# One block for attention and the gated stage, down products of six tiles chunk by chunk, and three x products placed right after the scan

## The chip, the core and the metric

The kernel runs on one core of a Trainium2 chip, in one launch. The metric is device time in microseconds. TensorE (PE, with its weight loads as PEld), VectorE (DVE), ScalarE (ACT), GpSimd (POOL) and SyncE (SP, which issues the transfers) run side by side and meet only at semaphores. The order of each engine's instructions is the order in which the Python code issues them.

## What is computed

1024 tokens (two sequences of 512) with 512 channels go through four stages. After each one its input is added and the sum is layer-normalised.

```
x = layernorm(x + mamba2(x))        # projections z, x, B, C; conv of 4 taps + silu; selective scan in 128-token
                                    # chunks, 8 groups; gating with silu(z); group norm; output projection
x = layernorm(x + x @ dequant(W))   # one 512x512 linear layer
x = layernorm(x + attention(x))     # 32 heads, 8 key/value heads, rotary, causal
g = silu(x @ gate.T * gs);  u = x @ up.T * us          # 1376 inner channels
x = layernorm(x + ((g * u) @ down.T) * ds)             # the gated stage
```

Operands that need more than 16 bits of mantissa are split in a leading and a remaining 16-bit half; a product of two such operands is three matmuls (lines 59, 60, 61), one with an exact operand two.

## The kernel before

**The mixer** (the first stage) works in *slots*. A tile is 128 of a group's 1024 channels for one sequence; there are 8 groups, 2 sequences, 8 tiles each, so 128 tiles, and a *unit* is the 8 tiles of one group and sequence. `slots` writes slot 0, then a loop over groups with slots 1 to 16, then the last 15 slots. In the slot of tile n TensorE does, in this order: `scan` of tile n (28 small float32 matmuls; the trace shows a float32 matmul as two) into bank 2; `states` of tile n+1 (3 float32 matmuls, 128x128) into bank 3; at a unit's first tile `sum_squares`; the x projection of tile n+3 (`project`, 12 matmuls of 128x512 in 16 bits, 4 k tiles of 3) into bank 0 or 1; `gate` of tile n+1 (12 such matmuls); `turn_x` of tile n+2 (4 transposes); at a unit's third and fifth tile the projection of B or C; `output` of tile n-1 (12 matmuls). The scans write and read the array in two halves of 64 columns (`128*64` in the rows); all else uses it whole (`128*128`).

Before the x projection TensorE waits in `free_bank` until the convolution has read the bank, and for the split of the weights (`wx_ok`). VectorE's slot begins with `u` (needs the scan), then `st` (copies the first chunk's state, needs `states`), `u*gz`, two more state steps, the masking of E for the next scan, the three convolution taps of tile n+3 with the remainder of y behind the first, and the scaling of the turned x. ScalarE's slot has, for even n, the exponentials of two tiles; then square and leading half of `u` (need `u*gz`), a copy of output weights (line 230, first sequence only), the first tap of the convolution (line 243, needs the x projection), eight decay instructions (line 984), a table load for odd n+1, and `gz` (line 1003), which the next scan needs. GpSimd makes xw and the decayed C, sums squares and splits weights; in the last unit it also prepares the linear layer's weights.

**Attention** (`attention`) ends with the output projection of the second sequence's four chunks, each followed on VectorE by an addition; chunks 0 to 5 are normalised, transposed by TensorE (`turn`, line 1416) and split in `xhi` and `xlo` there. Its `nc.Block()` ends with a barrier of all engines.

**The gated stage** (`swiglu`) is a block of its own. Per sequence it has 11 tiles of 128 inner channels (96 in the last), so 22 tiles n. TensorE takes `gate_up(n)` (8 matmuls gate, 8 up), then `down(n-1)`: 2 matmuls for each of 4 chunks of tokens, into banks 4 to 7. ScalarE takes `th` (silu), VectorE `h` = up * scale * th, ScalarE `hhi`, GpSimd `hlo`. Buffers are used in turn, two of each, and the tiles of a sequence run partly in a hardware loop. At a sequence's last tile VectorE scales the four banks (`down`) and adds to `resid`; for the first sequence all this stands ahead of the next tile's `h` on VectorE. Chunks 6 and 7 of the third layer norm are turned after `gate_up(0)`. For the last norm, GpSimd's `scale_and_shift` of chunks 0 to 3 stands behind the `hlo` of the last tile, and that of chunks 4 to 7 behind it. ScalarE then normalises and SyncE stores a chunk of 256 KB.

Of the kernel before, what the change touches and what calls it, by code (L numbers as in the profile page):

```python
# [6 lines left out]
F32 = mybir.dt.float32  # L7
# [119 lines left out]
class Scan:  # L127
# [105 lines left out]
    def project(self, w, b, bank, sem):  # L233
        k, x = self.k, slice(b * T, (b + 1) * T)
        for kt in range(KT):
            mm = product(self.nc, k.bank[bank][:, :], (lead(w[:, kt]), rest(w[:, kt])), (k.xhi[:, kt, x], k.xlo[:, kt, x]),
                         kt == 0, kt == KT - 1)
        mm.then_inc(sem, 1)
# [392 lines left out]
def mixer(k, io, sc, aw):  # L631
# [3 lines left out]
    with ExitStack() as tmp:  # L635
# [68 lines left out]
        with nc.Block() as block:  # L704
# [94 lines left out]
            def _(pe):  # L799
# [107 lines left out]
                def slot(g, m):  # L907
                    s = tile_at(g, m)
                    scan(s)
                    if tile_at(g, m + 1):  # L910
# [4 lines left out]
                    t = tile_at(g, m + 3)  # L915
                    if t:
                        free_bank(s)
                        pe.wait_ge(sc.wx_ok, t.g * CT + (t.i + 3))
                        sc.project(sc.wx[2 + t.i], t.b, ring_bank(s.b, x_use(s)), sc.xp_ready)
# [587 lines left out]
def attention(k, io, aw):  # L1507
# [3 lines left out]
    with ExitStack() as tmp:  # L1511
# [84 lines left out]

        with nc.Block() as block:
            @block.sync
            def _(sp):
# [19 lines left out]
                pairs(sp, body)  # L1619

            @block.tensor
            def _(pe):
# [113 lines left out]
                ln.turn(pe, 5, k.bank[4], N + 5)  # L1736

            @block.scalar
            def _(act):
# [63 lines left out]
                for t, bank in ((2, 4), (3, 2), (4, 3), (5, 4)):  # L1803
                    if t < 5:
                        ln.normalise(act, t + 1, N + t + 1)
                    ln.leading(act, t, k.bank[bank], N + t)

            @block.vector
            def _(dve):
# [101 lines left out]
                for t in range(CH):  # L1911
# [3 lines left out]
                    ln.remainder(dve, 2 + t, k.bank[(4, 2, 3, 4)[t]], N + 2 + t)  # L1915

            @block.gpsimd
            def _(pool):
# [58 lines left out]
                for t in range(CH - 1, 6):  # L1977
                    ln.scale_and_shift(pool, t, N + t)

# [73 lines left out]
def swiglu(k, out):  # L2053

    nc = k.nc
    with ExitStack() as tmp:
        def sb(name, shape, dt=F32):
            return k.sb(name, shape, dt, tmp)

        sc = sb("u_scale", [P, IT])
        th = [sb(f"th{i}", [P, T]) for i in range(2)]
        h = [sb(f"h{i}", [P, T]) for i in range(2)]
        hhi = [sb(f"hhi{i}", [P, T], F16) for i in range(2)]
        hlo = [sb(f"hlo{i}", [P, T], F16) for i in range(2)]
        add = [sb(f"down{i}", [P, HS]) for i in range(CH)]
        ln = k.norms[0]
        S = k.sem
        stored = S("stored")
        w = k.gated  # L2070
        gu_ok, d_ok, scales = w.gu_ok, w.d_ok, S("scales")
        g_ready, u_ready, d_ready = S("g_ready"), S("u_ready"), S("d_ready")
        silu_done, h_done, hi_done, lo_done = S("fsilu_done"), S("h_done"), S("fhi_done"), S("flo_done")
        scaled, added = S("fscaled"), S("fadded")

# [288 lines left out]
```

## Time and profile before

| | us |
|---|---|
| median of 3 runs | 2475.68 |
| lowest, highest | 2474.91, 2476.56 |
| profiled execution, its own time | 2477.49 |
| its span, first to last instruction | 2475.5 |

| engine | busy us (share) |
|---|---|
| TensorE matmuls | 2385.0 (96%) |
| TensorE weight loads | 1372.4 (55%) |
| VectorE | 1783.1 (72%) |
| ScalarE | 1591.1 (64%) |
| GpSimd | 1246.9 (50%) |

Matmuls are pipelined and their ends are modelled: a 128x512 matmul is drawn 0.38 us long, while the next one starts 0.216 us after it. So the cost of work on TensorE is read from one start to the next, never from the busy time. The mixer runs to about 1550 us of the span, the linear layer to 1598, attention to 2338, the gated stage to the end.

### The profile page before, as it was taken

The page shows a single profiled execution, that of the slowest core. Times are in us where ns is not written, and L with a number is a line of the kernel's source. Part 1 is how long each engine was busy: PE and PEld are TensorE (multiplying, and loading weights), DVE is VectorE, ACT ScalarE, POOL GpSimd, SP SyncE. Part 2 cuts the span into 40 slices and gives each one's busy share as a digit, 9 for nine tenths or more (in the row PEclk, how much of TensorE's full clock was granted, in tenths as well). Part 3 has the DMA queues.
Part 4 walks back from the last instruction along what each step waited for, and adds up shares of the span by engine and source line. Part 5 has one row for each costly group of instructions (what it writes and reads, how often), then busy time and mean ns, then how long its engine had stood idle before and what let it go on. Part 6 is the DMA issues. An engine that isn't in the chain of part 4 may idle for free. (4 is left out here: it accounts for less than half of the span.)

```text
span 2475.5 us, 49110 instructions
## 1 busy us (share of the span) xinstructions
PE 2385.0 (96%) x15624; PEld 1372.4 (55%) x15624; DVE 1783.1 (72%) x3234; ACT 1591.1 (64%) x3327; POOL 1246.9 (50%) x997
## 2 busy tenths in 40 slices
PE   6999999999999999999999998879999999999897
PEld 3555555555555555555555555445656555565443
DVE  5677777777777777777777776577787777878522
ACT  6676776766766776777777776256566656656422
POOL 4455556556556555556556549344444434444223
PEclk8999999999999999999999999999999999999999
DMA  7343343343343343333333342101110110121000
GB/s 246 100 133 108 107 137 109 102 140 110 102 136 115 102 135 110 108 128 116 109 122 118 129 127 81 52 36 43 43 44 1 44 44 1 43 78 38 1 0 34
DMA packets 113891, 218.79 MB, mean 88 GB/s; under 512 B 9696, under 2 KB 43104, under 8 KB 111424
## 3 DMA queue, kind: packets, MB, share of 16 engines
q1 hardware_dynamic: 113600, 215.28, 26.4%
q8 instruction: 137, 2.24, 0.4%
q14 instruction: 154, 1.26, 0.2%
HBM read 212.10 MB, written 3.15 MB: 87 GB/s over the span
## 5 line engine op out<-in xcount | busy, mean ns | idle before, releaser
L256 DVE SCALAR_TENSOR_TENSOR xc<-bank,taps,xc 128x511 f32<-128x511 f32 (+2 forms) x384 | 284.9, 742 | 48.5 <-ACT xc L243 31.4
L984 ACT ACTIVATE E<-wq,cst 128x128 f32<-128x128 f32 x1024 | 311.7, 389 | 2.4 <-PEq L298 2.4
L1277 POOL TENSOR_TENSOR acc<-acc,sq 128x512 f32<-128x512 f32 x112 | 177.0, 1581 | 188.0 <-ACT sq L996 188.0
L1268 POOL TENSOR_TENSOR xw<-xt,wdec 128x384 f32<-128x384 f32 x128 | 106.4, 831 | 316.2 <-DVE xt L1119 159.1
L1925 POOL TENSOR_TENSOR qT<-qT,qrot 128x512 f32<-128x512 f32 x64 | 81.2, 1269 | 350.1 <-DVE qrot L1815 350.1
L1161 DVE SCALAR_TENSOR_TENSOR u<-xc,D,bank 128x512 f32<-128x512 f32 x128 | 95.7, 747 | 210.7 <-PE bank L813 198.5
L60 PE MATMUL bank<-xlo,wx 128*128 128x512 f16 x640 | 243.1, 380 | 0.0
L59 PE MATMUL bank<-xhi,wx 128*128 128x512 f16 x640 | 243.1, 380 | 0.0
L61 PE MATMUL bank<-xhi,wx 128*128 128x512 f16 x640 | 242.9, 380 | 0.0
L1100 DVE TENSOR_TENSOR E<-E,cbm 128x1024 f32<-128x1024 f32 x128 | 236.7, 1849 | 0.8
L1263 POOL TENSOR_TENSOR ecs<-ecs,xcC 128x768 f32<-128x768 f32 x128 | 234.0, 1828 | 0.4 <-POOLq L298 0.4
L996 ACT ACTIVATE sq<-u 128x512 f32<-128x512 f32 x112 | 70.5, 630 | 230.8 <-DVE u L1166 230.8
L809 PE MATMUL bank<-E,xt 128*64 128x128 f32 x2048 | 186.7, 282 | 12.5 <-issue 9.1
L59 PE MATMUL bank<-xhi,wz 128*128 128x512 f16 x512 | 194.4, 380 | 0.2
L60 PE MATMUL bank<-wolo,yhi 128*128 128x512 f16 x512 | 194.3, 379 | 0.0
L59 PE MATMUL bank<-wohi,yhi 128*128 128x512 bf16 x512 | 194.3, 379 | 0.0
L60 PE MATMUL bank<-xlo,wz 128*128 128x512 f16 x512 | 194.3, 379 | 0.0
L61 PE MATMUL bank<-xhi,wz 128*128 128x512 f16 x512 | 194.3, 379 | 0.0
L61 PE MATMUL bank<-wohi,ylo 128*128 128x512 bf16 x512 | 194.3, 379 | 0.0
L1744 ACT ACTIVATE probs<-bank,nmx 128x512 f32<-128x512 f32 (+3 forms) x256 | 131.5, 526 | 54.7 <-DVE nmx L1845 54.7
L809 PEld LDWEIGHTS bank<-E,xt 128*64 128x64 f32 x2048 | 120.7, 138 | 58.6 <-issue 56.4
L813 PE MATMUL bank<-ecs,st 128*64 128x128 f32 x1536 | 152.3, 276 | 0.0
(239 smaller groups left out, 6340.2 us busy)
## 6 DMA issues: line engine op xcount, KB each, us to landing
wq<-cs_rows SPq DMA_DIRECT2D x128, 512.0 KB, 4.2
ecs<-ecs_rows SPq DMA_DIRECT2D x128, 384.0 KB, 3.5
wx<-in_w_xbc SPq DMA_DIRECT2D x80, 256.0 KB, 2.6
wz<-in_w_z SPq DMA_DIRECT2D x64, 256.0 KB, 2.7
wo<-in_w_o SPq DMA_DIRECT2D x64, 256.0 KB, 4.2
wq<-in_wq SPq DMA_DIRECT2D x8, 1024.0 KB, 5.7
awo<-in_wo SPq DMA_DIRECT2D x8, 1024.0 KB, 4.9
wkv<-in_wkv SPq DMA_DIRECT2D x8, 512.0 KB, 3.9
```

The source lines that it names most:

```text
L59: nc.tensor.matmul(out, lhs[0], rhs[0], start=first, stop=False, skip_group_check=skip)
L60: nc.tensor.matmul(out, lhs[0], rhs[1], start=False, stop=False, skip_group_check=skip)
L61: return nc.tensor.matmul(out, lhs[1], rhs[0], start=False, stop=last, skip_group_check=skip)
L256: self.nc.vector.scalar_tensor_tensor(out=dst[:, d:T], in0=self.k.bank[bank][:, 0:T - d], scalar=self.taps[:, bass.ds(g, 1), b, j, 3 - d:4 ...
L809: mm = nc.tensor.matmul(Y[r, cols], xt[t.i % 2][:, c, r], E[t.i % 4][:, h, c], start=True, stop=c == 0, skip_group_check=True)
L813: mm = nc.tensor.matmul(Y[r, cols], st[t.i % 2][:, c - 1, r], sc.ecs[t.i % 4][:, h, (c - 1) * P:c * P], start=False, stop=True, skip_group ...
L984: ins = nc.scalar.activation(E[t.i % 4][:, h, c], sc.csr[t.i % 2][:, h, c * P:(c + 1) * P], ACT.Relu, scale=-1.0, bias=head(sc.cst, t, c, h))
L1100: nc.vector.tensor_tensor(e, e, cbm[t.b][:].rearrange("p c t -> p (c t)").unsqueeze(1).to_broadcast([P, 2, T]), ALU.mult).then_inc(m_done, 1)
L1263: nc.gpsimd.tensor_tensor(e[:], e[:], sc.xcC[t.b][:, P:T].unsqueeze(1).to_broadcast([P, 2, T - P]), ALU.mult).then_inc(cs_done, 1)
L1268: nc.gpsimd.tensor_tensor(by_head(xw[t.i % 2][:]), by_head(xt[t.i % 2][:, 0:CH - 1]), of_heads(sc.wdec, t, 0, CH - 1), ALU.mult).then_inc( ...
L1277: nc.gpsimd.tensor_tensor(acc[t.b][:], acc[t.b][:], sq[:], ALU.add).then_inc(acc_done, 1)
L1744: ins = nc.scalar.activation(pr[h % 2][:, P_OFF[i]:P_OFF[i] + (i + 1) * P], k.bank[bank][:, at:at + (i + 1) * P], ACT.Exp, bias=nmx[h % 2] ...
```

## The change

Three things are done.

1. In a mixer slot, the first k tile of the x projection (3 of its 12 matmuls), with the two waits that stood ahead of it, is issued right after `scan`; then come `states` and `sum_squares`, then the other 9 matmuls.
2. The gated stage is a class whose parts are called at the end of each engine's part of the attention block. Its buffers are attention's (`th` is `qT`, `h` is `qrot`, the halves lie in the q, k and v halves, the scaled sums in `probs`). The barrier between is gone; TensorE instead waits for `proj_free` and for the third norm's `lo` counts where it needs a bank or a chunk. All 22 tiles are written out.
3. In the gated stage `down` follows by two tiles (`LAG`), chunks 6 and 7 are turned after `gate_up(1)`, the halves have 8 buffers (`RING`), and the down products of the last 6 tiles (`HELD`) are all taken after the last `gate_up`, chunk by chunk. The first sequence's scaling, adding, moments, and its `scale_and_shift` and normalisation stand at tiles 12, 13 and 14.

```diff
+                    t = tile_at(g, m + 3)
+                    def project_x(kts):
+                        sc.project(sc.wx[2 + t.i], t.b, ring_bank(s.b, x_use(s)), sc.xp_ready, kts)
+                    if t:
+                        free_bank(s)
+                        pe.wait_ge(sc.wx_ok, t.g * CT + (t.i + 3))
+                        project_x(range(0, 1))
                     if tile_at(g, m + 1):
                         states(tile_at(g, m + 1))
                     if s.i == 0 and not (isinstance(s.u, int) and s.u == 0):
                         pe.wait_ge(bt_done, s.u + 1)
                         sum_squares(1 - s.b, s.u, s.n)
-                    t = tile_at(g, m + 3)
                     if t:
-                        free_bank(s)
-                        pe.wait_ge(sc.wx_ok, t.g * CT + (t.i + 3))
-                        sc.project(sc.wx[2 + t.i], t.b, ring_bank(s.b, x_use(s)), sc.xp_ready)
+                        project_x(range(1, KT))
...
+LAG = 2
+HELD = 6
+RING = 8
...
+        def gate_up(n, b, i, rows):
+            if n == 0:
+                pe.wait_ge(w.gu_ok, 2 * KT)
+                pe.wait_ge(ln.lo, THIRD_NORM + CH)
+            if n < 2:
+                pe.wait_ge(self.proj_free, self.last_use + n)
+            else:
+                pe.wait_ge(self.silu_done, n - 1)
...
+            if n >= 2:
+                pe.wait_ge(self.h_done, n - 1)
...
+        held = NB * IT - HELD
+        for n, b, i, rows in self.tiles:
+            gate_up(n, b, i, rows)
+            if n == 1:
+                for t in (6, 7):
+                    ln.turn(pe, t, k.bank[t], THIRD_NORM + t)
+            if n == LAG:
+                pe.wait_ge(w.d_ok, DOWN_PIECES)
+                pe.wait_ge(ln.lo, LAST_NORM)
+            if 0 <= n - LAG < held:
+                for t in range(CH):
+                    down(n - LAG, t)
+        def held_products(t, a, b):
+            for n in range(held + a, held + b):
+                down(n, t)
+        held_products(0, 0, HELD - 1)
+        held_products(1, 0, HELD - 3)
+        held_products(0, HELD - 1, HELD)
+        held_products(1, HELD - 3, HELD)
+        held_products(2, 0, HELD)
+        held_products(3, 0, HELD)
...
+            if n == IT + LAG - 1:
+                for t in range(CH):
+                    scale(0, t)
+            if n == IT + LAG:
+                for t in range(CH):
+                    add_down(0, t)
+            if n == IT + LAG + 1:
+                dve.wait_ge(self.added, CH)
+                for t in range(CH):
+                    ln.moments(dve, t, LAST_NORM + t)
```

The order of instructions on TensorE in a slot of the mixer, from the scan on (lines 809 and 813, of the changed kernel 810 and 814); `x3` are the three matmuls of `states`. Before:

```order
L809 MATMUL bank<-E,xt 64x128 x2
L813 MATMUL bank<-ecs,st 64x128 x2
L818 REGISTER_ALU
L819 ISA
L821 MATMUL bank<-xw,bt 128x128 x3
L918 ISA
L59 MATMUL bank<-xhi,wx 128x512
```

After:

```order
L810 MATMUL bank<-E,xt 64x128 x2
L814 MATMUL bank<-ecs,st 64x128 x2
L888 ISA
L918 ISA
L59 MATMUL bank<-xhi,wx 128x512
L60 MATMUL bank<-xlo,wx 128x512
L61 MATMUL bank<-xhi,wx 128x512
L819 REGISTER_ALU
L822 MATMUL bank<-xw,bt 128x128 x3
```

Three x products and their two waits (`ISA`) have moved ahead of the states; behind the scan stands a 16-bit weight load instead of a float32 one.

TensorE from attention's last two transposed chunks (line 1416, after the change 1423) to the first gate product, before:

```order
L1416 MATMUL bank<-identity,resid 128x128 [waits n0_normed,n0_lo]
L1416 MATMUL bank<-identity,resid 128x128 x3
L1597 UNCONDITIONAL_BRANCH
L2098 UNCONDITIONAL_BRANCH [waits barrier_Pool_Activation_PE_DVE_SP_release]
L2109 MATMUL bank<-xhi,gatew 128x512 [waits gu_ok]
```

After:

```order
L1423 MATMUL bank<-identity,resid 128x128 [waits n0_normed,n0_lo]
L1423 MATMUL bank<-identity,resid 128x128 x3
L2117 MATMUL bank<-xhi,gatew 128x512 [waits aproj_free,n0_lo,gu_ok]
L2118 MATMUL bank<-xlo,gatew 128x512
L2117 MATMUL bank<-xhi,gatew 128x512
```

The barrier and two branches are gone; three counts of single semaphores stand in their place.

TensorE's last down products, before the change those of the last tile (`hhi1`, banks 4 to 7 are chunks 0 to 3):

```order
L2134 MATMUL bank4<-downw,hhi1 128x512 [waits flo_done,fhi_done]
L2136 MATMUL bank4<-downw,hlo1 128x512
L2134 MATMUL bank5<-downw,hhi1 128x512
L2136 MATMUL bank5<-downw,hlo1 128x512
L2134 MATMUL bank6<-downw,hhi1 128x512
L2136 MATMUL bank6<-downw,hlo1 128x512
L2134 MATMUL bank7<-downw,hhi1 128x512
L2136 MATMUL bank7<-downw,hlo1 128x512
```

After it, from the fifth held tile of chunk 0 to the last held tile of chunk 0 (`khi1`):

```order
L2138 MATMUL bank4<-downw,khi0 128x512 [waits flo_done,fhi_done]
L2140 MATMUL bank4<-downw,klo0 128x512
L2138 MATMUL bank5<-downw,qhi0 128x512
L2140 MATMUL bank5<-downw,qlo0 128x512
L2138 MATMUL bank5<-downw,qhi1 128x512
L2140 MATMUL bank5<-downw,qlo1 128x512
L2138 MATMUL bank5<-downw,qhi2 128x512
L2140 MATMUL bank5<-downw,qlo2 128x512
L2138 MATMUL bank4<-downw,khi1 128x512 [waits flo_done,fhi_done]
L2140 MATMUL bank4<-downw,klo1 128x512
```

Bank 4 is complete after these rows, with 15 pairs of products still to come, where before only the six matmuls of the other banks came after it.

## Rows read from the trace of the kernel before

**Rows 1.** Windows: stretch, length, busy (instructions) by engine, clock, DMA share, GB/s.
```profile
2340.80:2344.20 3.40, 3.38 (x9) 1.16 (x10) 2.08 (x7) 0.74 (x1) 2.04 (x5) 0.50 0.03 7
```

**Rows 2.** Timeline of TensorE, one slot: start, us, engine, line, what, [idle before].
```profile
800.36 0.39 PE L809 MATMUL bank<-E,xt 128*64 128x128 f32 x4
800.58 0.39 PE L813 MATMUL bank<-ecs,st 128*64 128x128 f32 x4
800.89 0.94 PE L821 MATMUL bank<-xw,bt 128*128 128x128 f32 x6
801.67 0.38 PE L59 MATMUL bank<-xhi,wx 128*128 128x512 f16 x1
801.88 0.38 PE L60 MATMUL bank<-xlo,wx 128*128 128x512 f16 x1
```

**Rows 3.** The same timeline, read from after the first of the six.
```profile
801.11 0.72 PE L821 MATMUL bank<-xw,bt 128*128 128x128 f32 x5
```

**Rows 4.** Timeline of TensorE where B times C stands before a scan.
```profile
787.15 1.05 PE L858 MATMUL bank<-xcC,xcB 128*128 128x128 f32 x8
788.14 0.66 PE L809 MATMUL bank<-E,xt 128*64 128x128 f32 x8
```

**Rows 5.** Timeline of TensorE, 16-bit products after an idle time, in attention.
```profile
1614.67 0.39 PE L59 MATMUL bank<-khi,qhi 128*128 128x512 f16 x1 [0.62 <-POOL qlo L1929]
1614.89 0.38 PE L60 MATMUL bank<-klo,qhi 128*128 128x512 f16 x1
```

**Rows 6.** Timeline of TensorE and VectorE, third tile of a unit.
```profile
835.12 0.94 PE L821 MATMUL bank<-xw,bt 128*128 128x128 f32 x6
836.09 0.29 DVE L1106 COPY st<-bank 128x128 f32<-128x128 f32 x1 [0.17 <-PE bank L821]
```

**Rows 7.** Timeline of ScalarE and then TensorE, seventh tile of a unit.
```profile
699.65 0.60 ACT L230 COPY wohi<-wo 128x512 bf16<-128x512 bf16 x1
700.32 0.78 ACT L243 ACTIVATE xc<-bank,taps 128x512 f32<-128x512 f32 x1
704.74 0.60 ACT L1003 ACTIVATE gz<-bank 128x512 f32<-128x512 f32 x1
706.00 0.66 PE L809 MATMUL bank<-E,xt 128*64 128x128 f32 x8
```

**Rows 8.** Timeline of TensorE at a scan, and of GpSimd in the last unit.
```profile
833.28 0.66 PE L809 MATMUL bank<-E,xt 128*64 128x128 f32 x8 [0.38 <-ACT gz L1003]
1498.90 0.83 POOL L1268 TENSOR_TENSOR xw<-xt,wdec 128x384 f32<-128x384 f32 x1 [0.99 <-DVE xt L1119]
```

**Rows 9.** Timeline from attention into the gated stage.
```profile
2336.95 1.04 PE L1416 MATMUL bank<-identity,resid 128*128 128x128 f32 x8
2340.81 0.69 DVE L1372 BATCH_NORM_STATS2 n_stats<-resid 128x6 f32<-128x512 f32 x1 [0.32 <-PEq L1597]
2340.82 0.59 PE L2109 MATMUL bank<-xhi,gatew 128*128 128x512 f16 x1 [2.83 <-PEq L1597]
2346.85 0.69 ACT L2171 ACTIVATE th<-bank,gs 128x512 f32<-128x512 f32 x1
2351.03 0.38 PE L2134 MATMUL bank<-downw,hhi 128*128 128x512 bf16 x1 [0.62 <-DVE xlo L1386]
```

**Rows 10.** Timeline of TensorE at the second sequence's first down product.
```profile
2411.00 0.38 PE L2134 MATMUL bank<-downw,hhi 128*128 128x512 bf16 x1 [2.82 <-issue]
```

**Rows 11.** Timeline of the end: last down product, VectorE, GpSimd.
```profile
2460.66 0.38 PE L2134 MATMUL bank<-downw,hhi 96*128 96x512 bf16 x1 [1.16 <-POOL hlo L2244]
2461.29 0.69 DVE L2210 TENSOR_TENSOR down<-bank,dscale 128x512 f32<-128x512 f32 x1 [2.65 <-PE bank L2136]
2463.57 0.67 DVE L2210 TENSOR_TENSOR down<-bank,dscale 128x512 f32<-128x512 f32 x1
2470.25 0.18 DVE L1376 BATCH_NORM_AGGREGATE n_mv<-n_stats 128x2 f32<-128x6 f32 x1
2471.03 0.23 POOL L1394 TENSOR_SCALAR n_rstd<-n_mv 128x1 f32<-128x1 f32 x1
```

More of the change, by code:

```diff
@@ L230, in lead_wo, with project @@
         self.nc.scalar.copy(self.wo_hi[i][:], lead(self.wo[i % 2][:])).then_inc(self.wo_lead, 1)
-    def project(self, w, b, bank, sem):
+    def project(self, w, b, bank, sem, kts=range(KT)):
         k, x = self.k, slice(b * T, (b + 1) * T)
-        for kt in range(KT):
+        for kt in kts:
             mm = product(self.nc, k.bank[bank][:, :], (lead(w[:, kt]), rest(w[:, kt])), (k.xhi[:, kt, x], k.xlo[:, kt, x]),
                          kt == 0, kt == KT - 1)
-        mm.then_inc(sem, 1)
+        if KT - 1 in kts:
+            mm.then_inc(sem, 1)
     def tap(self, act, q, bank, dst, g, b, j):
@@ L1504, in split_first_wo, with attention @@
         self.split_wo(0, 1)
-def attention(k, io, aw):
+def attention(k, io, aw, out):
     nc = k.nc
@@ L1595, in pairs, with flat @@
                 body(NG - 2 + s, s, NG // 2 - 1)
+        def flat(x):
+            return x[:].rearrange("p t d -> p (t d)")
+        gated = GatedStage(k, out, tmp, qT, qrot, [*qhi, *khi, *map(flat, vhi)], [*qlo, *klo, *map(flat, vlo)],
+                           [pr[t // 2][:, t % 2 * HS:t % 2 * HS + HS] for t in range(CH)], proj_free, LAST_OUT + CH - 1)
         with nc.Block() as block:
@@ L1619, in _ @@
                 pairs(sp, body)
+                gated.sync(sp)
             @block.tensor
@@ L1736, in _ @@
                 ln.turn(pe, 5, k.bank[4], N + 5)
+                gated.tensor(pe)
             @block.scalar
@@ L1806, in _ @@
                     ln.leading(act, t, k.bank[bank], N + t)
+                gated.scalar(act)
             @block.vector
@@ L1915, in _ @@
                     ln.remainder(dve, 2 + t, k.bank[(4, 2, 3, 4)[t]], N + 2 + t)
+                gated.vector(dve)
             @block.gpsimd
@@ L1978, in _ @@
                     ln.scale_and_shift(pool, t, N + t)
+                gated.gpsimd(pool)
 INTER = 1376
@@ L2250, in _ @@
                     ln.scale_and_shift(pool, t, LAST_NORM + t)
+        for t in range(CH, TT):
+            ln.scale_and_shift(pool, t, LAST_NORM + t)
 def program(nc, io, out):
@@ L2271, in program @@
                 aw.other_buffers(att)
-                attention(k, io, aw)
-            swiglu(k, out)
+                attention(k, io, aw, out)
 def layouts(i):
```

287 lines of the change are left out of this document (117 added, 170 removed).

## The prediction

> **What bounds the kernel now.** TensorE is busy 96% of the span in the table above, so in the mixer, where it has hardly an idle stretch, what can be gained is spacing: the distance from one matmul's start to the next. I read the windows of clock first (one low stretch, [rows 1]), then the timeline of TensorE in one slot of the mixer, then all engines' timeline at the two ends of the gated stage, where they do wait. The reader is to see three things. A 128x512 matmul takes 0.216 us (0.21 in the rows' two digits) from start to start [rows 2]; the change adds and removes none of them. Around the scan there are gaps that no wait explains. And the gated stage has a stretch at half clock, two stops and a long serial end.
>
> **Part 1, the x products behind the scan.** The scan's groups of four start 0.22 us apart (800.36, 800.58), so after the last four the array could go on at 800.80; the states start at 800.89. That is 0.09 us for leaving the 64-column form. The first state matmul then holds the array until 801.11, 0.22 us, while the other five take 0.56 together, 0.112 each [rows 2, 3]. So 0.10 us more is the float32 weight load, which nothing covers. Where float32 products of the same shape stand before a scan, the eight take 0.99, 8 x 0.112 and 0.09 for entering the 64-column form: behind a 16-bit matmul of 0.216 us their first load costs nothing [rows 4].
>
> After the change a 16-bit load stands in the exposed place. The nearest row is a restart in attention: first to second matmul 0.22 us, against 0.216 in a stream [rows 5]; read with more digits it is 0.01 more. So the slot loses the 0.10 and pays 0.01: a gain of 0.09. The drain stays, since something must be first after the scan. The bounds: 0 if the 16-bit load is as exposed as the float32 one; 0.19 if the drain too goes with the type of the load. I take 0.09, since the attention row is the same kind of load in an empty array.
>
> The Trainium skill bears on this in two places. TensorEngine Tiling (Array Packing), Key Properties, says that a change of tiling mode drains the engine; the 0.09 on both sides of the scan agree. Against the change speaks TensorE: Matmul & The Clock Gate, LDWEIGHTS: a load takes its number of columns over 1.2 GHz, whatever the type, an estimate of 0.107 us here, and by that alone the scan part would bring nothing (rival B). The same page's section on the weight path says that loads of types other than float32 go faster, and the restart row sides with that.
>
> How many slots keep it? 125 of 128 have an x projection. In the eight slots with the second tile of a group's first unit TensorE meets other limits (VectorE comes late behind the loop's jump; the next scan waits 0.38 us for gz, [rows 8]): nothing kept. In the last unit GpSimd has its last idle time at 1498.90 and from there works without a pause up to the last two scans, which wait for it [rows 8]; it is released there by VectorE, so what was gained before is kept (less up to 0.4, since VectorE runs later in its slot) and the three slots after it give nothing. Some 108 slots x 0.09 = 9.7, less 0.4: **9.3 us**.
>
> The cost is that the states come later by 0.66 (three x products), less the 0.10. They reach VectorE 0.97 us after their start: started at 835.12, st at 836.09, which already waited 0.17 there [rows 6]. In the common slot st starts 0.98 after the states' start without waiting, so it now comes about 0.55 later, and behind it u*gz, the state steps, the mask and the taps. Who waits for that? ScalarE's square and yhi. In the slot with the least room its copy wohi ends at 700.25 and the tap that needs the x projection starts at 700.32, so 0.07 of room; the tap comes 0.5 later, gz ends at 705.34 + 0.5, and the scan that needs it began at 706.00 [rows 7]: 0.66 of room, of which 0.1 is left, and the scan comes 0.09 sooner. That just fits; I count these seven slots (seventh tile, first sequence) at half. In the other slots with little room ScalarE waits for the x projection anyway by 0.6 to 1.4 us, and the projection ends no later than before. The moved waits (`free_bank`, `wx_ok`) now stand before the states in TensorE's queue, but VectorE has ended the last taps before a scan begins and GpSimd splits weights slots ahead, so they are met. SP's and GpSimd's own orders don't change here.
>
> **Part 2, one block.** TensorE ends the transposes of chunks 4 and 5 at 2336.95 + 8 x 0.109 = 2337.82 and starts the gate products at 2340.82 [rows 9]: 3.0 us. The bank, chunks 0 to 3 and the weights are ready by 2336, so it goes on at once. Then 3.4 us at clock 0.50, the level of 1.2 GHz [rows 1], in which the work of 1.7 us is done: 1.65 lost; they follow the idle time and I let them go with it.
>
> But the stage's start is a chain: moments of chunk 6 on VectorE at 2340.81, which waited 0.32 for the barrier, GpSimd, two normalisations, a table load, th at 2346.85 to 2347.54 [rows 9]. All that comes only 0.3 sooner. After the change TensorE does gate_up(0) (3.45, 16 x 0.216) to 2341.3, gate_up(1) to 2344.7, turns 6 and 7, the last behind the normalisation at 2345.3, to 2345.8, and then waits for silu(0), some 2347.35: **a new wait of 1.5 us**. gate_up(2) ends 2350.8, when the remainder of chunk 7 is ready too (before 2351.03, now 0.3 sooner), and down(0) starts. Before, down(0) started at 2351.03 after two gate_ups, now after three: 3.7 us gained.
>
> **Part 3, the order of down.** In the second sequence's start TensorE stopped 2.82 us (2411.00, [rows 10]) behind VectorE's eight scale and add instructions, which stood ahead of h. With a lag of two tiles (5.18 us each) and these spread over three tiles, none is late: four normalisations on ScalarE behind GpSimd's chain hold silu(15) to about 10 us after h(14), and up(17), which needs h(15), comes at 12. Gain 2.98 (start to start 3.20 less 0.216). Before the last down TensorE stopped 1.16 [rows 11], start to start 1.32; now 8 pairs, 3.45, stand between the last up and the first product of the last tile, whose halves need 3.05 (2460.66 less 2457.61, the start of the tile before). Gain 1.32.
>
> The end: let X be the end of the last gate_up. X = 2337.82 + 22 x 3.453 + 0.87 (turns) + 1.55 (the new wait) + 16 x 1.726 (downs taken by then) = 2443.8. Chunk 0 has 9 pairs ahead, its last pair starts at X + 3.45; VectorE's scale starts 0.63 after that (2460.66 to 2461.29), X + 4.08. VectorE takes 2.28 a chunk (2461.29 to 2463.57), less than the 2.59 of six pairs, so the last aggregate ends 9.14 later (2461.29 to 2470.43), X + 13.2; the last chunk's products are ready at X + 10.55, VectorE comes to them at X + 10.9. From there, without the queue that GpSimd had before (2470.43 to 2471.03), 0.1 and then 4.51 (2471.03 to the span's end at 2475.54) [rows 11]. End: 2443.8 + 13.2 + 4.6 = 2461.6, **13.9 us sooner**. 8.2 of it are stops on TensorE, the rest is that VectorE starts 6.3 us ahead of TensorE's end where it started 1.1 ahead.
>
> **The sum.** 9.3 + 13.9 = 23.2. The span goes from 2475.5 to 2452.3. The profiled execution took 2477.49 in all, 2.0 more than its span, and 1.8 more than the median 2475.68; I take the gain from the median: **2452.5 us**.
>
> **Rivals.** A is the forecast, 2450 to 2456 with what each term can miss by; chance 0.57.
> B: the 16-bit load is exposed like the float32 one, 0.10 a slot. Against it speaks the restart [rows 5]; for it, that no row shows such a load right behind a scan. The mixer keeps its time: 2475.7 - 13.9 = 2461.8; chance 0.18.
> C: the drain goes too (it belongs to the float32 load). 108 x 0.19 = 20.5: 2441; the same 0.09 before the scan, where no such load is exposed in front, speaks against; 0.05.
> D: the late states get through to some of the scans with little room (third, seventh and first tiles, about 0.25 in each of 24), or the new wait in the gated stage brings half clock behind it (1.65 more). 2456 to 2460; 0.12.
> E, slower: the 0.55 us on VectorE and ScalarE reaches the next scan in every slot. That decides from the point at which gz is later than TensorE, that is, when ScalarE's room of about 0.7 to 2.9 is gone. If it were, 125 x 0.55 = 69 less 23 and plus 9 lost: 2530. The room in rows 7 speaks against; 0.03.
> F, the change does nothing: all engines' chains at the ends refill what is saved. The stops are in the rows, so 0.03. Remaining 0.02: elsewhere.
>
> **How the numbers follow.** The predicted time is A's. From 2447 to 2463.5 lie A, B and D with their own spread, 0.85. A measurement of this kernel can tell about 0.2%, 5 us. Faster by more: A to D, 0.93. Within: F and bad cases of D, 0.04. Slower: 0.03.
>
> **What would show it.** In the slot: the first x product 0.2 after the scan's last pair, the next one 0.22 behind it (B: 0.31), the six state halves all 0.112 apart, the common slot 10.66 instead of 10.75. `st` on VectorE waiting some 0.5 for the states in most slots. The last two scans waiting for GpSimd still. At the front: gate products from about 0.2 after the transposes, clock 1.00, one stop of 1.5 before the third tile. No stop at the second sequence's first down. The last store 18 us after the last up product. It would be wrong if the second x product comes 0.31 after the first, if gz starts to be waited for in the slots of rows 7 by more than 0.1, or if the 22 written-out tiles show stops that the loop didn't have.

## The result, and the profile after

The changed kernel takes **2453.44 us** (median of 4 runs, 2450.45 to 2455.02), against 2475.60 for the kernel before (4 runs, 2474.91 to 2476.56). The ratio is 0.9903, with a 95% interval of 0.9891 to 0.9915: 22.2 us, or 0.97%. The forecast was 2452.5. The profiled execution took 2454.91, with a span of 2452.9.

The first section of the page of the kernel after:

```profile
PE 2371.0 (97%) x15624; PEld 1371.9 (56%) x15624; DVE 1799.8 (73%) x3234; ACT 1582.3 (65%) x3327; POOL 1235.6 (50%) x997
```

The matmul count is what it was; the span around it is shorter. Where, can be read in the same places as before.

**One slot of the mixer.** Timeline of TensorE behind a scan (columns as in [rows 2]: start, duration, engine, line, what, count):

```profile
794.74 0.39 PE L814 MATMUL bank<-ecs,st 128*64 128x128 f32 x4
795.06 0.39 PE L59 MATMUL bank<-xhi,wx 128*128 128x512 f16 x1
795.29 0.38 PE L60 MATMUL bank<-xlo,wx 128*128 128x512 f16 x1
795.51 0.38 PE L61 MATMUL bank<-xhi,wx 128*128 128x512 f16 x1
795.72 0.83 PE L822 MATMUL bank<-xw,bt 128*128 128x128 f32 x6
796.39 0.38 PE L59 MATMUL bank<-xhi,wx 128*128 128x512 f16 x1
```

From the last scan group to the first x product it is 0.32 us, and it was 0.31 to the first state product in [rows 2]: the drain is still there. From first to second x product it is 0.23 (0.227 in the median of 125 slots), to the third 0.22 (0.216). The six state products take 0.67 together (795.72 to 796.39), where they took 0.78 in [rows 2]. In the median of all slots the first of them holds the array 0.109 us instead of 0.213. The common slot is 10.66 us long instead of 10.75, and every other form of slot that waits for nobody is shorter by the same 0.09 (11.47 for 11.56, 13.25 for 13.34, 10.99 for 11.08, 11.55 for 11.64).

The price shows on VectorE, in the same slot:

```profile
796.59 0.29 DVE L1113 COPY st<-bank 128x128 f32<-128x128 f32 x1 [0.56 <-PE bank L822]
796.80 0.68 DVE L1173 TENSOR_TENSOR u<-u,gz 128x512 f32<-128x512 f32 x1
```

It waits 0.56 us for the states where in common slots it waited for nothing. ScalarE's square starts 4.13 us after the scan's start instead of 3.58 (medians).

**The gated stage.** Timeline of all engines from attention into it (answers [rows 9]; the tiles of the gated stage now carry names of attention's buffers, qT for th, qhi for hhi):

```profile
2328.20 1.04 PE L1423 MATMUL bank<-identity,resid 128*128 128x128 f32 x8
2329.08 0.38 PE L2117 MATMUL bank<-xhi,gatew 128*128 128x512 f16 x1
...
2334.22 0.81 ACT L1411 ACTIVATE resid<-resid,n_shift,n_rstd 128x512 f32<-128x512 f32 x1 [4.31 <-POOL n_shift L1405]
2335.55 0.82 ACT L1411 ACTIVATE resid<-resid,n_shift,n_rstd 128x512 f32<-128x512 f32 x1 [0.51 <-POOL n_shift L1405]
2336.38 1.28 ACT L2177 ACT_TABLE_LOAD   x1
2337.68 0.69 ACT L2177 ACTIVATE qT<-bank,gs 128x512 f32<-128x512 f32 x1
...
2338.42 0.39 PE L2117 MATMUL bank<-xhi,gatew 128*128 128x512 f16 x1 [1.34 <-ACT qT L2177]
2341.88 0.38 PE L2138 MATMUL bank<-downw,qhi 128*128 128x512 bf16 x1
```

The gate products follow the transposes after 0.88 us instead of 3.87, and no matmul there has the 0.63 us of half clock. The new wait stands where the forecast put it, before the third tile, with 1.34 us. It is the only wait of TensorE from here to the end: the stops of [rows 10] and of the last down product in [rows 11] are gone.

**The end.** Timeline of TensorE's last up product, then VectorE's scale of the first two chunks and last aggregate, GpSimd, ScalarE (answers [rows 11]):

```profile
2434.91 0.38 PE L2127 MATMUL bank<-xlo,upw 128*96 128x512 f16 x1
...
2439.21 0.69 DVE L2215 TENSOR_TENSOR probs<-bank,dscale 128x512 f32<-128x512 f32 x1 [3.09 <-PE bank L2140]
2441.49 0.67 DVE L2215 TENSOR_TENSOR probs<-bank,dscale 128x512 f32<-128x512 f32 x1
...
2448.17 0.18 DVE L1383 BATCH_NORM_AGGREGATE n_mv<-n_stats 128x2 f32<-128x6 f32 x1
2448.44 0.23 POOL L1401 TENSOR_SCALAR n_rstd<-n_mv 128x1 f32<-128x1 f32 x1 [0.90 <-DVE n_mv L1383]
2449.72 0.81 ACT L1411 ACTIVATE resid<-resid,n_shift,n_rstd 128x512 f32<-128x512 f32 x1 [1.33 <-POOL n_shift L1405]
```

X, the end of the last gate_up, is 2435.12. VectorE begins 4.09 later, takes 2.28 for the first chunk, and ends its last aggregate at 2448.35, X + 13.2; the span ends at 2452.95, X + 17.8. All three are the forecast's figures.

### The profile page after: what moved, and what is told of

Read it like the earlier page. It is cut to its first block and busy times, and to the rows that moved or that the text cites. A ratio compares the mean times of both kernels' runs of the same rounds, so it can differ in the third digit from the quotient of the medians.

```text
span 2452.9 us, 48815 instructions
## 1 busy us (share of the span) xinstructions
PE 2371.0 (97%) x15624; PEld 1371.9 (56%) x15624; DVE 1799.8 (73%) x3234; ACT 1582.3 (65%) x3327; POOL 1235.6 (50%) x997
## 3 DMA queue, kind: packets, MB, share of 16 engines
q8 instruction: 139, 2.28, 0.4%
## 5 line engine op out<-in xcount | busy, mean ns | idle before, releaser
L1284 POOL TENSOR_TENSOR acc<-acc,sq 128x512 f32<-128x512 f32 x112 | 163.9, 1464 | 190.0 <-ACT sq L1003 190.0
```

The costliest lines, as they stand in the source:

```text
L1284: nc.gpsimd.tensor_tensor(acc[t.b][:], acc[t.b][:], sq[:], ALU.add).then_inc(acc_done, 1)
```

## Times by stage

Runs of one and the same kernel differ here by up to 8 us, more than several of the effects that are to be told apart. So each profiled execution was also cut at four starts of TensorE: the first scan, the last scan, the first k/v product of attention (wkv), and the last transposes before the gated stage. In brackets stands the time that the stretch spent at a granted clock of 0.50 (the 1.2 GHz level).

```
kernel                     to scan 0    scan 0 - last   last - wkv   wkv - transposes  transposes - end   span
before                     61.3 (17.7)  1486.6 (13.0)   50.3 ( 4.9)    738.7 (25.8)     138.6 (11.9)     2475.5
after                      60.9 (16.0)  1476.5 ( 8.7)   52.0 (11.1)    738.8 (25.7)     124.7 ( 5.1)     2452.9
after, second profile      60.7 (16.7)  1476.8 (14.1)   50.4 ( 7.8)    736.4 (19.5)     124.7 ( 5.3)     2449.0
x products only            60.5 (16.1)  1478.4 (11.2)   52.2 (10.7)    736.3 (20.0)     138.6 (11.8)     2466.0
gated part only            61.2 (14.0)  1483.9 ( 9.9)   52.2 (10.7)    736.5 (20.1)     124.8 ( 4.9)     2458.4
32 columns ahead           59.7 (12.6)  1487.0 ( 7.9)   50.6 ( 7.3)    736.5 (20.0)     124.8 ( 5.0)     2458.5
one product ahead          60.9 (14.8)  1475.0 (12.5)   50.5 ( 7.7)    737.8 (23.0)     124.8 ( 3.2)     2448.9
twelve products ahead      60.3 (15.6)  1549.1 (11.7)   50.6 ( 7.6)    736.6 (23.1)     124.7 ( 5.3)     2521.3
SiLU first                 61.2 (15.9)  1479.1 (11.4)   52.1 (11.1)    739.4 (26.5)     123.2 ( 3.4)     2455.1
block apart                60.8 (16.4)  1476.5 ( 7.5)   50.6 ( 7.5)    734.8 (16.4)     128.0 ( 6.7)     2450.6
down tile by tile          59.9 (14.4)  1478.7 ( 9.5)   50.6 ( 7.6)    736.6 (23.1)     129.9 (10.5)     2455.6
one ahead and SiLU first   60.5 (16.1)  1474.3 (11.2)   50.8 ( 8.6)    738.7 (25.6)     123.2 ( 3.5)     2447.5
```

The attention column is the same work in all twelve, and it differs by 4.7 us. Windows of that stretch in the shortest ("block apart") and in the longest ("SiLU first"): bounds, length, busy time and count of PE, PEld, DVE, ACT and POOL, granted clock, DMA share, GB/s.

```profile
1587.85:2322.62 734.77, 705.31 (x4628) 418.45 (x4689) 566.48 (x1231) 431.30 (x1131) 315.57 (x261) 0.99 0.11 40
```

```profile
1592.41:2331.84 739.43, 713.98 (x4689) 421.65 (x4690) 566.80 (x1231) 431.20 (x1131) 315.53 (x261) 0.98 0.11 39
```

## The experiments

**1. The first part alone.** The kernel before with

```
+                    if t:
+                        free_bank(s)
+                        pe.wait_ge(sc.wx_ok, t.g * CT + (t.i + 3))
+                        project_x(range(0, 1))
                     if tile_at(g, m + 1):
                         states(tile_at(g, m + 1))
...
-                        sc.project(sc.wx[2 + t.i], t.b, ring_bank(s.b, x_use(s)), sc.xp_ready)
+                        project_x(range(1, KT))
```

> The kernel before with the first part of the change alone: of x projection's twelve matmuls the first three stand ahead of the next states' products, the gated stage and its block stay as they were. If the two parts are independent, and the 9 us that the mixer and attention stages gained come from the three matmuls alone: 2475.6 - 8.8 = 2466.8 us, and the common slot 10.66 us instead of 10.75. If the gain came through the changed gated stage (code or tiles laid out otherwise): 2475.6 us, slots of 10.75.

Measured: 2470.33 us (8 runs, 2467.96 to 2472.49) against 2476.36 before on the same chip (12 runs, 2473.71 to 2482.03), ratio 0.9974, interval 0.9964 to 0.9985. The gain is there without the new gated stage, with a common slot of 10.66. But it is 6.0 us and not 8.8. In the table two places stand out: the mixer gained 8.2 where the kernel after gained 10.1, and the 50 us behind it took 1.9 more, with 10.7 us at half clock instead of 4.9, much as in the kernel after. Of the mixer's difference of 1.9, 1.3 us is in the slots with the seventh tile of the first sequence: 11.26 us on average over the six of the second to seventh group, where it could be 10.99 (1.6 us), and the kernel after has 11.03. The next scan waits for gz in some of them (below, in 6). The rest is in the slots with the first and second tile, whose length differs between executions of every kernel here. The profile itself, the fastest of the eight runs, is 9.6 us below that of before, 2.4 of it in attention, which the change doesn't touch.

**2. The second part alone.** The kernel after with the x products where they were:

```
-                        project_x(range(0, 1))
...
-                        project_x(range(1, KT))
+                        project_x(range(KT))
```

> The kernel after with the whole of x projection behind the next states' products again, as before; only the second part of the change (attention and gated stage in one block, the last six down products chunk by chunk) is left. Independent parts: 2475.6 - 13.9 = 2461.7 us, slots of 10.75, first states' product 0.21 after the scan's end. If the parts interact (the granted clock, which set the spread of 4 us between runs of the kernel after, is better only with both): anything from 2464 to 2467.

Measured: 2462.38 us (5 runs, 2460.35 to 2463.13), 14.0 below before; forecast for this part 13.9. The stage takes 124.75 us against 138.59, the same as in the kernel after, and the slots are 10.75 again. So the first part changes nothing in the second's stage. The mixer takes 1483.9 us against 1486.6 before, although nothing in it was changed: 2.6 of these 2.7 us are in the slots with a second tile (1.6 of them in one slot, which before spent 3.4 us at half clock). So much a mixer differs without any change.

**3. How many products ahead.** Ahead of the states stands the first product alone; the other eleven stand behind them:

```
+        if part == 0:
+            one(0, lead(w[:, 0]), k.xhi, 0, ahead, True, False)
+            return
...
-                        project_x(range(0, 1))
+                        project_x(0)
```

> The kernel after with one matmul of x projection (the first, 512 columns, 16-bit weights) ahead of the states' products instead of three; the other eleven come behind them. My theory: what is saved is the float32 weight load that stood bare behind the scan, 0.10 us, and any one matmul of 0.22 us covers it: 2453.4, within 1 us, the common slot 10.66, and the states 0.43 us earlier than with three (0.12 us later than before), so that VectorE's and GpSimd's margins are wider; up to 0.5 us less is possible for that. Rival, that the work ahead pays by keeping TensorE fed while it waits for VectorE and ScalarE, so that more of it is better: about two thirds of the 8.8 us lost, 2459.

Measured: 2451.49 us (4 runs, 2450.89 to 2451.60). Timeline of TensorE in the slot, and at the scan of a slot in the last unit:

```profile
795.39 0.39 PE L247 MATMUL bank<-xhi,wx 128*128 128x512 f16 x1
795.62 0.83 PE L842 MATMUL bank<-xw,bt 128*128 128x128 f32 x6
796.29 0.38 PE L247 MATMUL bank<-xlo,wx 128*128 128x512 f16 x1
...
1486.33 0.66 PE L830 MATMUL bank<-E,xt 128*64 128x128 f32 x8
```

One 512-column product covers the load as well as three: the states take 0.67 and the common slot 10.66. The rival (more work ahead is better) is out. By the medians it can't be told from three ahead (2453.4, and 2451.0 in experiment 9), and it lies below what I had expected. By the stage it is better than three, by more than the 0.5 that I had allowed: from first to last scan it takes 1475.0 us, and the six profiles with three ahead take 1476.5 to 1479.1. The kernel after waits for gz at the same scan of the last unit:

```profile
1487.19 0.66 PE L810 MATMUL bank<-E,xt 128*64 128x128 f32 x8 [0.56 <-ACT gz L1010]
```

With one ahead the square starts 3.70 us after the scan's start, with three 4.13, and this 0.43 is what the tight slots lack.

**4. Is it the cover, or the type of the first load?** Ahead of the states stand 32 of the first product's 512 columns; the other 480 follow behind them as a matmul of their own:

```
+        if ahead < T:
+            one(0, lead(w[:, 0]), k.xhi, ahead, T, False, False)
...
+                        sc.project_parts(sc.wx[2 + t.i], t.b, ring_bank(s.b, x_use(s)), sc.xp_ready, part, 32)
```

> The kernel after, but ahead of the next states' products stand only 32 of the 512 columns of x projection's first matmul; its other 480 columns come behind them, as a thirteenth matmul, and then the remaining eleven. Theory of the cover (the float32 load of the first states' product stands bare unless a matmul of 0.216 us runs ahead of it): 32 columns are 0.014 us long and cover nothing, so the load of about 0.10 us is bare again, the common slot is 10.75 to 10.78 us and the run 2462 to 2466 us. Theory of the first load (what counts is that the load behind the scan is of a 16-bit type, whatever follows it): the gain of 0.09 a slot stays, the common slot is 10.66 to 10.69 and the run 2452 to 2456 us.

Measured: 2460.80 us (4 runs, 2460.45 to 2466.13), common slot 10.76, as the theory of the cover has it; the run is 1.2 us under its lower end, with attention at 736.5 us. Timeline of TensorE:

```profile
800.13 0.19 PE L247 MATMUL bank<-xhi,wx 128*128 128x32 f16 x1
800.17 0.92 PE L842 MATMUL bank<-xw,bt 128*128 128x128 f32 x6
800.92 0.37 PE L247 MATMUL bank<-xhi,wx 128*128 128x480 f16 x1
```

The 32 columns start right behind the scan and are over in 0.04; then the six state products take 0.75 instead of 0.67, the first of them 0.193 us (median of all slots; 0.109 with three ahead). The float32 load is bare again by 0.08; the rest of the 0.10 that the slot is longer is the split matmul, whose two parts take 0.24 instead of 0.23. So it is the cover: what runs ahead must last long enough. Two lengths were tried, 0.04 us, which leaves 0.08 bare, and 0.22, which leaves nothing; how much would just do was not. The type of the load right behind the scan matters too, but only for what is left bare there: 0.10 us with float32, 0.01 with 16 bits.

**5. All twelve ahead.**

```
-                        project_x(range(0, 1))
+                        project_x(range(KT))
...
-                    if t:
-                        project_x(range(1, KT))
```

> The kernel after with all twelve matmuls of x projection ahead of the next states' products. TensorE itself has no more and no less to do than with three, and the load is covered just as well: if nobody waited for the states it would be 2453 us. My theory is that the room behind the states is spent: with three ahead ScalarE's square starts 4.13 us behind the scan's start, with twelve at 4.13 + 9 x 0.216 = 6.07; the chain square, tap, gz then ends after 11.3 us instead of 8.9, and in the common slot of 10.66 us TensorE waits for gz some 0.8 us, in the tight slots (gz already within 0.7 us) 1.6 us: about 13 us in 16 slots, 2550 us in all, range 2500 to 2600.

Measured: 2523.29 us (one run). TensorE's work is the same as in the kernel after, and the mixer is 72.6 us longer. Timeline of ScalarE in the slot whose scan starts at 829.94, and of the next scan:

```profile
836.01 0.63 ACT L1001 ACTIVATE sq<-u 128x512 f32<-128x512 f32 x1 [5.29 <-DVE u L1171]
836.55 0.71 ACT L1004 ACTIVATE yhi<-u,nw 128x512 f16<-128x512 f32 x1
837.16 0.77 ACT L244 ACTIVATE xc<-bank,taps 128x512 f32<-128x512 f32 x1
...
840.17 0.57 ACT L1008 ACTIVATE gz<-bank 128x512 f32<-128x512 f32 x1
840.89 0.66 PE L810 MATMUL bank<-E,xt 128*64 128x128 f32 x8 [0.22 <-ACT gz L1008]
```

The square comes at 6.07, to the digit as expected, and the scan waits for gz. The forecast of 2550 was too high by 27 us. It had 13 us in 16 slots, and the mixer lost 9. Six of the 16 lost nothing: the slots of 13.25 and 11.55 us were longer than the chain's 11.3 already. And ScalarE's copy wohi (0.5) stands in the chain of the first sequence alone: there the common slot is 11.46 us, as expected, and in the second sequence it is 10.94. Of the tight slots the seventh tile's lost 1.9 instead of 1.6. This prices rival E of the prediction: with the states late enough the change turns into a loss of 46 us.

**6. The new wait.** ScalarE takes the first SiLU ahead of the normalisations of chunks 6 and 7, and the second ahead of their leading parts:

```
-        for t in (6, 7):
-            ln.normalise(act, t, THIRD_NORM + t)
...
-            silu(n, b, i, rows)
+            if n != 1:
+                silu(n, b, i, rows)
+            if n == 0:
+                for t in (6, 7):
+                    ln.normalise(act, t, THIRD_NORM + t)
             leading_h(n, rows)
             if n == 0:
+                silu(*self.tiles[1])
```

> The kernel after with ScalarE's orders at the start of the gated stage changed: the first SiLU stands ahead of the normalisations of chunks 6 and 7, the second SiLU ahead of their leading parts. If the wait of 1.34 us at the third gate product comes from the first SiLU standing behind the two normalisations, it goes: 2453.4 - 1.3 = 2452.1 us. Rival: the turns of chunks 6 and 7 now wait for the normalisations that come later, 0.5 to 1.5 us, and nothing is won: 2453.4, or up to 1 us more.

Measured: 2452.69 us (4 runs, 2450.52 to 2457.03). Timeline of ScalarE, then of TensorE:

```profile
2334.68 1.28 ACT L2177 ACT_TABLE_LOAD   x1 [1.13 <-PE bank L2118]
2335.97 0.69 ACT L2177 ACTIVATE qT<-bank,gs 128x512 f32<-128x512 f32 x1
2337.86 0.81 ACT L1411 ACTIVATE resid<-resid,n_shift,n_rstd 128x512 f32<-128x512 f32 x1 [1.20 <-POOL n_shift L1405]
2339.18 0.81 ACT L1411 ACTIVATE resid<-resid,n_shift,n_rstd 128x512 f32<-128x512 f32 x1 [0.51 <-POOL n_shift L1405]
...
2339.61 1.09 PE L1423 MATMUL bank<-identity,resid 128*128 128x128 f32 x8
2340.54 0.38 PE L2117 MATMUL bank<-xhi,gatew 128*128 128x512 f16 x1
```

The table load and the SiLU fit into the time in which ScalarE waited for GpSimd anyway (4.31 us in the kernel after). The normalisations come no later: 6.02 us behind the transposes in both kernels. TensorE has no wait left in the whole stage, which takes 123.24 us instead of 124.75. The 1.5 us can't be read from the median: it lies 0.8 us below the first of the kernel after and 1.7 above the second (experiment 9), and the four runs spread over 6.5. The profiled execution was the slowest of the four, and its mixer the longest of the six with three products ahead (1479.1 us). Timeline of ScalarE and TensorE behind the seventh tile's slot there:

```profile
702.03 0.60 ACT L1010 ACTIVATE gz<-bank 128x512 f32<-128x512 f32 x1
702.78 0.66 PE L810 MATMUL bank<-E,xt 128*64 128x128 f32 x8 [0.35 <-ACT gz L1010]
```

The same slot of the kernel after had gz at 700.11 and the scan at 700.89, without a wait. On average over the second to seventh group this slot takes 11.35 us here, 11.26 in experiment 1, 11.27 in experiment 8, 11.01 to 11.05 in the other three with three ahead, and 10.99 and 11.00 with one ahead. So the same code falls into this wait in some executions and not in others. Where the scan waits, it starts 0.14 us after gz has ended, in every profile: so long the hand-over takes. In the slots of the kernel after that don't wait it starts 0.16 to 0.18 after it, so that only 0.02 to 0.04 us is left (with one ahead 0.61, so 0.47, and before 0.66, so 0.52). A small delay is enough; what makes it differ I have not found.

**7. The block.** The kernel after with the gated stage in a block of its own:

```
-                gated.tensor(pe)
...
+        with nc.Block() as block:
+            @block.tensor
+            def _(pe):
+                gated.tensor(pe)
```

(and so for the other four engines.)

> The kernel after with the gated stage in a block of its own again, so that the engines meet between attention and it; code, buffers and the order of the down products stay as after. My terms: the idle time at the meeting was 3.0 us of TensorE and brought 1.65 us of half clock, but with the meeting the new wait of 1.3 us at the third gate product partly goes (the normalisations of ScalarE run meanwhile): 2453.4 + 3.0 + 1.65 - 0 to 1.3 = 2456.7 to 2458. Rival, that the meeting cost nothing by itself and the gated stage's gain is all from its end: 2453.4.

Measured: 2454.53 us (4 runs, 2452.61 to 2457.12). Timeline of TensorE, and the window of low clock:

```profile
2322.62 1.04 PE L1423 MATMUL bank<-identity,resid 128*128 128x128 f32 x8
2326.63 0.38 PE L2133 MATMUL bank<-xhi,gatew 128*128 128x512 f16 x1 [2.97 <-PEq L1610]
```

```profile
2327.90:2331.30 3.40, 3.40 (x9) 1.21 (x8) 0.69 (x5) 1.71 (x3) 2.08 (x5) 0.50 0.00 0
```

Both come back, the idle time and the half clock behind it. It begins 1.3 us after TensorE has started again; before the change it began with the restart (2340.80, [rows 1]). The stage takes 128.00 us instead of 124.75: 3.1 idle and 1.5 at half clock, less the new wait of 1.3, which is gone. That is 3.25, at the low end of what I expected. The median is only 1.1 above the first of the kernel after, and so under the range that I gave, and 3.5 above the second. In this profile, the fastest of its four runs, attention took 4 us less. By the first median alone the block would have been called nearly free.

**8. The order of the last down products.**

```
-        held_products(0, 0, HELD - 1)
...
-        held_products(3, 0, HELD)
+        for n in range(held, NB * IT):
+            for t in range(CH):
+                down(n, t)
```

> The kernel after with the down products of the last six tiles taken tile by tile (each over all four chunks) instead of chunk by chunk. TensorE does the same work; the four sums close within the last tile instead of one after another. VectorE, 2.28 us a chunk, can then begin about 10.2 us after the last up product ends (12 x 4 matmuls of 0.216) instead of 4.1, so that its four chunks stand behind TensorE: last output about 4.6 us behind the last aggregate, at 10.2 + 4 x 2.28 + 4.6 = 24 us against 17.8, less the half clock's share: 5 to 6.5 us slower than the kernel after, 2458.5 to 2460. Rival, that the chunk order brings nothing since VectorE's work was hidden or the end is set by the stores: 2453.4.

Measured: 2455.49 us (4 runs, 2454.57 to 2457.57). Timeline of the last up product, and of VectorE's first scale and last aggregate:

```profile
2432.39 0.38 PE L2127 MATMUL bank<-xlo,upw 128*96 128x512 f16 x1
...
2441.88 0.69 DVE L2208 TENSOR_TENSOR probs<-bank,dscale 128x512 f32<-128x512 f32 x1 [8.26 <-PE bank L2140]
...
2450.83 0.18 DVE L1383 BATCH_NORM_AGGREGATE n_mv<-n_stats 128x2 f32<-128x6 f32 x1
```

VectorE starts at X + 9.3 instead of X + 4.1, and the span ends at X + 23.0 instead of X + 17.8: the chunk order is worth 5.2 us. I had put the stage's loss at 5 to 6.5 (VectorE comes a little before the 10.2 that I gave). The median is 2.0 above the first of the kernel after, 3 us under the range that I gave, and 4.5 above the second.

**9. The kernel after once more, and both finds together.**

> The kernel after once more, with more runs, so that the others stand beside it on one chip. Its median 2453.4 within 1.5 us; in its profile the stages that nothing changed (attention, 739 us; the stretch between the last scan and attention, 52 us) differ from the first profile by the time spent at half clock alone, about 0.45 us for each us of it.

Measured: 2451.01 us (4 runs, 2449.36 to 2456.77), 2.4 below the first median, where I had allowed 1.5. In the second profile attention took 736.4 us with 19.5 at half clock, against 738.8 with 25.7: 0.4 us for each.

> The kernel after with both gains of the first runs: one matmul of x projection ahead of the states instead of three, and ScalarE's first two SiLU ahead of the normalisations and leading parts of chunks 6 and 7. One ahead gave 1.9 us (2451.5 against 2453.4), the SiLU order 1.5 us in the gated stage (124.75 to 123.24). If both hold together: 2450.0, within 1 us. If the 1.9 was only how the half clock fell in those runs: 2451.9.

Measured, on the same chip: **2448.52 us** (4 runs, 2446.60 to 2449.46), ratio to before 0.9883, interval 0.9866 to 0.9899. It is the fastest of the series, 1.5 us below what I expected and 2.5 below the kernel after, whose interval (0.9884 to 0.9918) its own overlaps. Its stages say the same more sharply: 1474.3 us in the mixer against 1476.8, and 123.2 in the gated stage against 124.7.

## Why the prediction was right, point by point

The forecast of 2452.5 lies between the two medians of the kernel after, 2453.4 and 2451.0 (experiment 9).

**The x products.** The step from float32 to 16-bit load was sized right: 0.213 became 0.109 at the states and 0.216 became 0.227 at the first x product, 0.09 a slot in the balance. Rival B would have shown a second x product 0.31 after the first; it comes after 0.23. The rule that gives a load's time by its columns alone (the Trainium skill, TensorE: Matmul & The Clock Gate, LDWEIGHTS), on which B leaned, does not hold here: 0.10 us of the float32 load was bare, and 0.01 of the 16-bit load. The trace also draws the loads themselves apart, the first float32 load of the states behind a 16-bit load in the kernel after:

```profile
795.29 0.10 PEld L61 LDWEIGHTS bank<-xhi,wx 128*128 128x128 f16 x1
795.51 0.19 PEld L822 LDWEIGHTS bank<-xw,bt 128*128 128x128 f32 x1
```

Both have 128 columns; one is drawn 0.10 us long and the other 0.19. C fell too, since the drain is still there: 0.31 from the last scan group to what follows it before, 0.32 after. Experiment 4 shows what I had only argued, that it is a cover.

**How many slots keep it.** Here the total was near with some luck. From the first to the last scan the kernel after gained 10.1 us, where I had 9.3. (It is 10.56 ahead at the last scan; 0.43 of that it had at the first, in a stretch that the change doesn't touch.) 104 slots are shorter by 0.09 each, 9.4 in all. The prediction's 108 was close to that, though its own counts (125 less 8, less 3, less half of 7) give 110.5. The slots with the first to third and the seventh tile of a first unit bring 2.1 more, 1.7 of it in one slot that spent 3.4 us at half clock before and none after. That can't be put down to the change: the slots with the second tile, which I had written off, took 10.75 to 11.06 us on average in the six profiles with three products ahead (second to seventh group), and 11.02 and 10.85 in the two with the old order, so whether they keep the 0.09 is not shown. In the last unit I had put the loss at up to 0.4, and it was 1.3: 11.90 ahead at scan 122, 10.56 at scan 127. Two of its scans now wait for gz (0.56 above, and 0.16), and the two that wait for GpSimd are still there, the first of them longer than before, as this row of the kernel after shows:

```profile
1522.95 0.91 PE L810 MATMUL bank<-E,xt 128*64 128x128 f32 x6 [5.45 <-issue]
```

Then 1.7 went in the 50 us behind the mixer, at half clock for 11.1 us instead of 4.9, and 8.75 were left at the last transposes. The other experiments show that this 1.7 comes and goes whatever the kernel (both single parts had it, the second profile of the same kernel did not).

**The late states.** "That just fits" did not hold even in the profile of the kernel after. The delay was as sized (0.56 at st), but two of the eight slots with least room take 11.26 us instead of 10.99, with the scan waiting 0.21 for gz, which the prediction had named as a sign of being wrong (over 0.1). The room was counted up to the end of gz, and 0.14 of it belongs to the hand-over (experiment 6): of what I thought left, 0.02 to 0.04 us was. In the kernel after that cost 0.3 us in the second to seventh group; in three of the six profiles with three products ahead it costs 1.6 to 2.2. Rival D had this at 2456 to 2460 as a case of its own; it is rather a part of the forecast's spread, and it goes with one product ahead.

**One block.** 3.0 idle and 1.65 of half clock were forecast; put back alone, they brought 3.1 and 1.5. The new wait was put at 1.5 and is 1.34, in the place and for the reason named. It brought no half clock behind it.

**The order of down, the stops, the end.** X was forecast at 2443.8 less the gain before it; with 8.75 that is 2435.05, and it is 2435.12. VectorE's start (X + 4.08), the last aggregate (X + 13.2) and the end (X + 17.8) hold to 0.1 us, and the stage's gain is 13.84 against 13.9. Of this the block (3.25) and the chunk order (5.2) were taken back one at a time. The rest, 5.4, was not tested by itself and is read from the rows: the stops at 2351.03, 2411.00 and 2460.66 of the kernel before (start to start 0.78, 2.98 and 1.32 us above the 0.216 of a stream, 5.1 in all) are gone. Apart from the new wait, none of the 22 written-out tiles shows a stop that the loop didn't have.

## What to carry over

A float32 weight load behind a change of tiling mode stood bare here by 0.10 us; one full 16-bit matmul ahead of it hid it, 32 columns didn't, and more than one only delayed whoever waits for what was pushed back. An engine that waits for a slow chain can do its next independent job first: ScalarE's SiLU ahead of two normalisations cost nothing in its stage and freed TensorE. Room before a wait has to be counted less the hand-over, 0.14 us here. And where a kernel's runs spread as widely as the effect, cut each profile into stages: the block barrier cost 3.3 us in its stage, and 1.1 or 3.5 by the medians, according to which of the two of the same kernel it is held against.

## What the runs showed of the chip that I had not expected

- The time at half clock differs between executions of the same code: in attention 16.4 to 26.5 us, each worth 0.46 us of time, 4.7 us in all. That is more than half of the widest spread between runs of one kernel (8.3 us, the kernel before in experiment 1). In the mixer, where TensorE hardly stops, no profile shows any from 80 us on until the idle times before the last two scans.
- A matmul of 32 columns behind the scan takes 0.04 us with its 16-bit load, and the float32 load behind it is still bare by 0.08 of the 0.10 us.
- A slot whose margin is 0.02 to 0.04 us beyond the hand-over is nearly stable in one execution (11.01 us on average) and not in another (11.35). What tips it stays open.
